# Self attention of a decoder layer: scores by 32-row query strips, probabilities turned by VectorE in 32x32 blocks, values contracted by 32 keys on four row strips

## The chip, the cores and the metric

The kernel runs on one core of one Trainium2 chip. The time is the device time of one execution in microseconds (us), median of three runs. A core has TensorE (PE in the profile, its weight loads PEld), VectorE (DVE), ScalarE (ACT), GpSimd (POOL) and SyncE (SP), which issues most DMAs. Each engine works through its own queue in order and waits on semaphores for the others.

## The reference

One post-norm decoder layer on 8 batches of 112 tokens and 256 channels, all in float32. The first third, self attention with 16 heads of 64 channels and no mask, is what changes:

```python
qkv = x @ w_qkv                                   # (8, 112, 256) @ (256, 3072)
q, k, v = split(qkv, 3)                           # 16 heads of 64
attn = softmax(einsum('bhid,bhjd->bhij', q, k) / 8)
out = einsum('bhij,bhjd->bhid', attn, v) @ w_out + b_out
x = layernorm(x + out)
```

Behind it come cross attention over 375 context rows (16 heads of 16 channels, masked), layer norm, then a mixture of 8 experts with one expert per token beside a shared one, and the last layer norm.

## The kernel before

The program is written as one instruction list for each engine; the order in a list is the order of the work, and every hand-over is a semaphore.

Self attention goes batch by batch (the loop `for b in range(B)` of each engine). Of each batch it takes 16 heads in four groups `g` of four heads; two groups, which hold the even and the odd heads of a pair of row halves, are a `pair`. On TensorE, batch `b` is, in order:

- `score1(0, b)` (L465): 8 matmuls, 64 channels by 112 queries as weights, 112 keys moving; even and odd heads use the two row halves of the array and two PSUM banks.
- from batch 2 on, `out1(b - 2)` (L504): the output projection of a tile of 128 tokens, 8 matmuls of 256 columns.
- `between1(b, 0)` and, from batch 2 on behind `score1(1, b)`, `between1(b, 1)`: two halves of the value projection of the next batch (`project_v1`, L448), each 2 matmuls of 512 columns.
- `turn(g, b)` (L477) for the four groups, with `between1(b, 2)` to `between1(b, 5)` behind each: four query/key projections for the next pair of batches (`project_qk`, L434). In batch 6 these are key and value projections of cross attention (L526, L532), in batch 7 transposes of x1, projections of cross attention's queries, values and keys (L511, L532, L518, L526).
- `value1(0, b)`, `value1(1, b)` (L491): 16 matmuls, 112 keys by 64 channels as weights, 112 queries moving.

A turn is four PE transposes of 112x112 probabilities into bank 4. All projections share banks 2 and 3 (`PE_J1`) in turns, so each waits until the bank's last content has been evacuated: value projections by ScalarE (`evac_v`, L930), query/key projections by VectorE (`evac_qk`, L1098).

On VectorE a batch is: row maxima (`rowmax`, L1105), normalisation of the probabilities with the reciprocal of their sum (`normalise`, L1111 and L1113), copies of the turned probabilities out of PSUM (`evac_pt`, L1119), the evacuations of the query/key projections, and the two parts of layer norm (`ln1_a`, L1124 to L1131, which waits for the output projection; `ln1_b`, L1139). On ScalarE a batch is: exponentials of groups 0 and 1 (`exps`, L938, four activations of 112 columns each), `evac_v(0, b + 1)`, exponentials of group 2, `evac_v(1, b + 1)`, exponentials of group 3, and two evacuations of the attended values (`evac_o`, L944).

GpSimd takes the root of the layer norm (L349) and fills constants at the start. SyncE's loads are all issued from its own list; the expert weights follow the last output projection.

A float32 matmul leaves two MATMUL and two LDWEIGHTS records in the trace, a PE transpose one.

## Time and profile before

| what | us |
|---|---|
| median of three runs (lowest, highest) | 437.46 (437.05, 437.85) |
| span of the profiled execution, first to last instruction | 436.2 |
| one batch in self attention (first score block of batch 3 to that of batch 4) | 18.55 |
| busy time of TensorE over the span | 414.0 (95%) |

The profiled execution's own time is not listed apart from its span; it is one execution of the same program as the three timed runs. Blocks of the last two batches that the next sections use, from the timeline of TensorE: a key projection 1.28 (138.32 to 139.60), a value projection of cross attention 0.98 (141.64 to 142.62), the query projection 1.54.

The page gives for each engine its busy time and share; the chain that ended last is followed back from the last instruction through whatever released each step. In the timeline each row is one or several like instructions: start, time until the last of them ended, engine, line, operation, output and inputs, shapes, and in brackets how long the engine had been idle and who ended it. A matmul's end is modelled, so the start of the next block says more on how long a block holds TensorE than its own length.

### The profile page before, as it was taken

Reading aid. Unit: us, or ns where it says so; the run is one execution under the profiler, and the core shown is the slowest. Engines: PE = TensorE matmul, PEld = TensorE weight load, DVE = VectorE, ACT = ScalarE, POOL = GpSimd, SP = SyncE. Lnnn points to the kernel's source line nnn. Section 1 sums busy time; section 2 is a strip of 40 time slices with the busy share of each in tenths; the row PEclk is TensorE's granted clock in tenths of the full one; section 3 lists DMA queues with packets and bytes.
Section 4 is the critical chain, followed back from the end, with each engine's and each line's share of the span. In section 5 each row is a group of like instructions: output and inputs, shape, how many; then the busy total and the mean of one; then the engine's idle time right before and its main releaser. Section 6 shows DMA issues by size and latency. Waiting matters only on the chain.

```text
span 436.2 us, 8958 instructions
## 1 busy us (share of the span) xinstructions
PE 414.0 (95%) x3125; PEld 297.5 (68%) x3126; DVE 243.9 (56%) x724; ACT 194.1 (45%) x580; POOL 50.9 (12%) x77
## 2 busy tenths in 40 slices
PE   8999999999999979999999999999989999999992
PEld 7767869778796856776766676767665474666661
DVE  1365765747466556666665666667762552244442
ACT  1064452433526446677666666767673101111110
POOL 4010010100101001000010101010100045212222
PEclk9999999999999999999999999999999999999999
DMA  8998100000000013040404131910000013122111
GB/s 246 365 385 242 21 2 2 0 2 2 1 2 0 2 37 145 2 181 13 170 17 166 53 130 43 387 43 2 2 2 2 1 50 109 48 62 69 67 38 31
DMA packets 15241, 34.22 MB, mean 78 GB/s; under 512 B 2381, under 2 KB 9150, under 8 KB 13920
## 3 DMA queue, kind: packets, MB, share of 16 engines
q1 hardware_dynamic: 13952, 30.70, 20.2%
q0 software_dynamic: 1104, 2.76, 1.8%
q8 instruction: 25, 0.41, 0.4%
q10 hardware_dynamic: 144, 0.23, 0.2%
q14 instruction: 16, 0.13, 0.1%
HBM read 27.24 MB, written 6.70 MB: 78 GB/s over the span
## 4 chain that ended last, share of the span: by engine, by line
PE 83%; DVE 6%; ACT 4%; issue 3%; POOL 2%; DMA 1%; POOLq 0%; DVEq 0%; ACTq 0%
PE bank L434 11%; PE bank L633 10%; PE bank L448 7%; PE bank L615 6%; PE bank L504 6%; PE bank L532 5%; PE bank L649 4%; PE bank L879 4%; PE bank L855 4%; PE bank L861 4%; PE bank L526 3%; PE bank L465 3%; PE bank L789 3%; PE bank L491 3%; PE bank L477 3%
## 5 line engine op out<-in xcount | busy, mean ns | idle before, releaser
L1234 DVE CUSTOM_DVE_ANT_0 p<-bank,mask 112x375 f32<-112x375 f32 x128 | 62.7, 545 | 36.5 <-PE bank L615 36.5
L995 ACT ACTIVATE p<-p,nm 112x375 f32<-112x375 f32 x128 | 74.8, 609 | 2.0 <-DVE nm L1234 2.0
L633 PEld LDWEIGHTS bank<-ident,p 112*125 112x125 f32 x384 | 48.9, 187 | 22.9 <-issue 14.5
L1002 ACT ACTIVATE pT<-bank 125x336 f32<-125x336 f32 x96 | 42.8, 447 | 46.0 <-PE bank L633 46.0
L633 PE MATMUL bank<-ident,p 112*125 112x112 f32 x384 | 58.8, 286 | 1.0
L434 PE MATMUL bank<-x2T,arena 128*128 128x224 f32 x256 | 54.6, 362 | 0.0
L938 ACT ACTIVATE p<-bank,nm 112x112 f32<-112x112 f32 x128 | 43.5, 365 | 18.3 <-DVE nm L1105 18.3
L434 PEld LDWEIGHTS bank<-x2T,arena 128*128 128x128 f32 x256 | 47.8, 195 | 1.0 <-DMA x2T<-in_xT 0.7
L349 POOL TENSOR_TENSOR rstd<-veps,minus_half 128x1 f32<-128x1 f32 x14 | 7.7, 549 | 292.2 <-DVE veps L1131 292.2
L1105 DVE TENSOR_REDUCE nm<-bank 112x4 f32<-112x448 f32 x32 | 19.2, 620 | 24.1 <-PE bank L465 24.1
L1098 DVE TENSOR_SCALAR arena<-bank 128x448 f32<-128x448 f32 x32 | 19.9, 623 | 22.7 <-PE bank L434 22.7
L615 PE MATMUL bank<-kT,qz 32*112 32x375 f32 x256 | 28.8, 517 | 3.6 <-ACT x2T L964 2.1
L448 PE MATMUL bank<-arena,x2T 128*112 128x512 f32 x64 | 30.2, 602 | 0.0
L944 ACT ACTIVATE arena<-bank 128x448 f32<-128x448 f32 x16 | 8.7, 544 | 48.1 <-PE bank L491 48.1
L938 ACT ACTIVATION_READ_ACCUMULATOR p<-bank,nm 112x1 f32 x128 | 27.9, 218 | 0.0
L532 PE MATMUL bank<-wx,mid 128*125 128x256 f32 x96 | 26.5, 399 | 0.0
L504 PE MATMUL bank<-arena 128*128 128x256 f32 x112 | 26.0, 385 | 0.3 <-DVE qscale L1161 0.3
L789 PE MATMUL bank<-x2T,ugs 128*128 128x512 f32 (+1 forms) x64 | 25.5, 544 | 0.6 <-DVE pT L1315 0.4
L1072 ACT ACTIVATE p<-bank 128x512 f32<-128x512 f32 x9 | 5.4, 597 | 44.9 <-PE bank L855 44.9
L649 PE MATMUL bank<-pT,v 125*32 125x112 f32 x768 | 25.0, 263 | 0.0
L649 PEld LDWEIGHTS bank<-pT,v 125*32 125x32 f32 x768 | 17.3, 109 | 10.1 <-issue 7.4
L504 PEld LDWEIGHTS bank<-arena 128*128 128x128 f32 x112 | 20.7, 190 | 4.1 <-ACT arena L944 0.5
(140 smaller groups left out, 596.5 us busy)
## 6 DMA issues: line engine op xcount, KB each, us to landing
arena<-in_ug SPq DMA_DIRECT2D x8, 1024.0 KB, 5.7
arena<-in_dn SPq DMA_DIRECT2D x8, 512.0 KB, 7.1
mid<-in_ctxT SPq DMA_DIRECT2D x8, 375.0 KB, 3.1
slots_s<-blank SPq DMA_DIRECT2D x14, 128.5 KB, 4.0
arena<-in_wqk SPq DMA_DIRECT2D x7, 256.0 KB, 5.8
slots_x<-blank SPq DMA_DIRECT2D x14, 128.0 KB, 6.1
p<-slots_s SPq DMA_DIRECT2D x9, 128.5 KB, 2.0
kT<-slots_x SPq DMA_DIRECT2D x9, 128.0 KB, 2.1
```

The source lines that it names most:

```text
L434: mm = pe.matmul(J[:, m * S_PAIR:(m + 1) * S_PAIR], wqk[:, 2 * u + m, k, :], xT[:, i, k, :], start=(k == 0), stop=(k == KC - 1))
L448: mm = pe.matmul(PE_J1[c][0:S, :], xT[:, b // 2, k, (b % 2) * S:(b % 2 + 1) * S], wv1[:, c, k, :], start=(k == 0), stop=(k == KC - 1))
L504: mm = pe.matmul(PE_W1[:, 0:C], oT1[:, k, t * TILE:(t + 1) * TILE], wout[:, k, :], start=(k == 0), stop=(k == 7))
L532: mm = pe.matmul(M[0:SK, 0:C], ctxT[:, b % 2, k, t * SK:(t + 1) * SK], wx[:, 2, k, :], start=(k == 0), stop=(k == KC - 1))
L615: mm = pe.matmul(PE_S2[r][0:S, 0:S2], qz[rows_r, b // 2 % 2, m, par, b % 2, :], kT2[rows_r, b % 2, m, :], start=True, stop=True)
L633: mm = pe.transpose(PE_T2[r][0:SK, t * S:(t + 1) * S], p2[i % RING][:, t * SK:(t + 1) * SK], ident[0:S, 0:S])
L649: mm = pe.matmul(PE_V2[VP * r:VP * r + VP, g * S:(g + 1) * S], v2[:, b % 2, t, g * STRIPS + r, :], pT2[0:SK, (n * STRIPS + r) % RING, t, : ...
L789: mm = pe.matmul(bank[2 + 2 * (n % 2) + part][:, 0:width(grp)], ugs[:, k, part * HID + m * 128:part * HID + (m + 1) * 128], x2T[:, k, grp ...
L938: e = act.activation(p1[g][:, n, :], PE_S1[g % 2][0:S, n * S:(n + 1) * S], ACT.Exp, bias=nm1[:, h:h + 1], accum_out=rs1[:, h:h + 1])
L995: act.activation(p2[i % RING], p2[i % RING], ACT.Exp, bias=nm2[:, i % H:i % H + 1], scale=-1.0).then_inc(exp2, 1)
L1002: act.activation(pT2[0:SK, i % RING], PE_T2[r][0:SK, 0:KT * S].rearrange("p (k n) -> p k n", k=KT), ACT.Copy).then_inc(pt2_act, 1)
L1234: v.tensor_tensor_reduce(p2[i % RING], PE_S2[r][0:S, 0:S2], bias[:], 1.0, 3e38, ALU.add, ALU.min, accum_out=nm2[:, i % H:i % H + 1]).then_ ...
```

## The change

Scores (`score1`): instead of one matmul per head with all 112 queries, a head gets four, one for each block of 32 queries (16 in the last). A head's strip of 32 PSUM partitions is its place among four, so a bank holds four heads by strips of 32 query rows and, side by side, the four query blocks. The two row halves of the array are used as before.

Softmax: row maxima, exponentials, reciprocals and the multiply now run over 128 partitions (four heads by 32 queries) and four query blocks, in as many instructions as before. The columns 112 to 127 of each block are zeroed once by GpSimd.

Turn: the PE transposes and the copies out of PSUM are gone. In their place VectorE transposes each group's 128x512 probabilities in 32x32 blocks from SBUF to SBUF (`turn_blocks`), with keys of a head on its strip of 32 partitions.

Values (`value1`): the contraction runs over 32 keys at a time, on four row strips of the array, accumulated over four key blocks in one PSUM bank per strip. The values are projected in the matching layout (`project_v1`): strips of 32 tokens as weights, 256 columns moving, two of four token blocks per bank; the columns of the value weights are reordered on the way in.

PSUM: the value blocks take banks 4 to 7, with the output projection in the upper half of bank 7; an evacuation of attended values reads one half of all four banks. Order on TensorE: `between1(b, 0)` moves ahead of the output projection, the turns drop out. Order on VectorE: row maxima 2 and 3 stand behind the first transpose and `normalise(1)`, and the query/key evacuations are spread between the rest (`drain1`).

The diff, cut to its core:

```diff
-        v1 = [carve(INNER)[0:S] for _ in range(2)]
+        v1 = [carve(INNER).rearrange("p (j n) -> p j n", j=QB) for _ in range(2)]
...
 
-        p1 = [p2_all[0:S, j * G1 * S:(j + 1) * G1 * S].rearrange("p (k n) -> p k n", k=G1) for j in range(4)]
-        pT1 = [pT_all[0:S, j * G1 * S:(j + 1) * G1 * S].rearrange("p (k n) -> p k n", k=G1) for j in range(4)]
+        p1_all = p2_all[:, 0:4 * QB * 128].rearrange("p (g i n) -> p g i n", g=4, i=QB)
+        p1 = [p1_all[:, g] for g in range(4)]
+        pT1 = [pT_all[:, g * QB * 128:(g + 1) * QB * 128].rearrange("p (j n) -> p j n", j=QB) for g in range(4)]
...
 
-        PE_S1, PE_J1, PE_T1, PE_U1, PE_W1 = bank[0:2], bank[2:4], bank[4], bank[5:7], bank[7]
+        PE_S1, PE_J1, PE_U1, PE_W1 = bank[0:2], bank[2:4], bank[4:8], bank[7][:, 256:512]
+        U1_ALL = banks[:, 4 * 512:8 * 512].rearrange("p (c n) -> p c n", c=STRIPS)
         PE_S2, PE_V2, PE_M2 = bank[0:STRIPS], bank[5], bank[6]
         PE_T2 = (bank[4], bank[7], PE_S2[0], PE_S2[1])
         PE_L2 = PE_S2[2]
 
-        def head1(g, n):
-
-            return 2 * G1 * (g // 2) + 2 * n + g % 2
+        def block1(j, full=True):
+
+            return SQ if full or (j + 1) * SQ <= S else S - j * SQ
...
             g.memset(ones[:], 1.0).then_inc(consts, 1)
+            g.memset(p1_all[:, :, :, S:128], 0.0).then_inc(padded1, 1)
...
             def project_v1(b, c):
+
                 if b == 0:
-                    pe.wait_ge(w_v[c], 16)
+                    for half in range(2):
+                        pe.wait_ge(w_v[half], 16)
                     pe.wait_ge(qk_sb, 7 + c)
                 elif b == 1:
                     pe.wait_ge(v1_sb, c + 1)
                     pe.wait_ge(xT_loaded[1], 16)
                 else:
                     pe.wait_ge(qk_sb, 4 * b + 3 + c)
-                for k in range(KC):
-                    mm = pe.matmul(PE_J1[c][0:S, :], xT[:, b // 2, k, (b % 2) * S:(b % 2 + 1) * S], wv1[:, c, k, :],
-                                   start=(k == 0), stop=(k == KC - 1))
+                if (b, c) == (3, 0):
+                    pe.wait_ge(prep, 7)
+                for j in (2 * c, 2 * c + 1):
+                    m = block1(j, b % 2 == 0)
+                    at = (b % 2) * S + j * SQ
+                    for k in range(KC):
+                        for strip in range(STRIPS):
+                            mm = pe.matmul(PE_J1[c][SQ * strip:SQ * strip + m, (j % 2) * 256:(j % 2) * 256 + 256],
+                                           xT[:, b // 2, k, at:at + m], wv1[:, strip // 2, k, (strip % 2) * 256:(strip % 2) * 256 + 256],
+                                           start=(k == 0), stop=(k == KC - 1))
                 mm.then_inc(v1_pe, 1)
 
...
                 cols_b = slice((b % 2) * S, (b % 2 + 1) * S)
-                for n in range(G1):
-                    for g in (2 * pair, 2 * pair + 1):
-                        h = head1(g, n)
-                        r = slice(64 * (h % 2), 64 * (h % 2) + 64)
-                        mm = pe.matmul(PE_S1[g % 2][0:S, n * S:(n + 1) * S], qT[b // 2 % 2][r, h // 2, cols_b],
-                                       kT[b // 2 % 2][r, h // 2, cols_b], start=True, stop=True)
-                        if n == G1 - 1:
-                            mm.then_inc(scores1[g], 1)
-
-            def turn(g, b):
-                if b == 0:
-                    pe.wait_ge(consts, 4)
-                pe.wait_ge(norm1, b * 4 + (g + 1))
-                if b * 4 + g >= 1:
-                    pe.wait_ge(pt1, b * 4 + g)
-                for n in range(G1):
-                    mm = pe.transpose(PE_T1[0:S, n * S:(n + 1) * S], p1[g][:, n, :], ident[0:S, 0:S])
-                mm.then_inc(turn1, 1)
+                for i in range(QB):
+                    m = block1(i, b % 2 == 0)
+                    at = (b % 2) * S + i * SQ
+                    for strip in range(STRIPS):
+                        for par in range(2):
+                            r = slice(64 * par, 64 * par + 64)
+                            mm = pe.matmul(PE_S1[par][SQ * strip:SQ * strip + m, i * 128:i * 128 + S],
+                                           qT[b // 2 % 2][r, 4 * pair + strip, at:at + m],
+                                           kT[b // 2 % 2][r, 4 * pair + strip, cols_b], start=True, stop=True)
+                            if (i, strip) == (QB - 1, STRIPS - 1):
+                                mm.then_inc(scores1[2 * pair + par], 1)
 
             def value1(pair, b):
 
-                pe.wait_ge(pt1, b * 4 + (2 * pair + 2))
+                pe.wait_ge(turned1, b * 4 + (2 * pair + 2))
                 if pair == 0:
                     pe.wait_ge(v1_sb, 2 * b + 2)
                 if b >= 1:
-                    pe.wait_ge(ot1[pair], b)
-                for n in range(G1):
-                    for g in (2 * pair, 2 * pair + 1):
-                        h = head1(g, n)
-                        col = (h // 2 % 4) * S
-                        mm = pe.matmul(PE_U1[pair][64 * (h % 2):64 * (h % 2) + 64, col:col + S],
-                                       v1[b % 2][:, h * D1:(h + 1) * D1], pT1[g][:, n, :], start=True, stop=True)
+                    pe.wait_ge(ot1[0], b)
+                    pe.wait_ge(ot1[1], b)
+                if b >= 2:
+                    pe.wait_ge(y1, b - 1)
+                for j in range(QB):
+                    n = block1(j, False)
+                    for par in range(2):
+                        at = (2 * pair + par) * D1
+                        for strip in range(STRIPS):
+                            rows_s = slice(SQ * strip, SQ * strip + n)
+                            mm = pe.matmul(PE_U1[strip][64 * par:64 * par + 64, pair * S:(pair + 1) * S],
+                                           v1[b % 2][rows_s, j, at:at + D1], pT1[2 * pair + par][rows_s, j, 0:S],
+                                           start=(j == 0), stop=(j == QB - 1))
                 mm.then_inc(pv1[pair], 1)
 
             def out1(t):
...
                     pe.wait_ge(w_loaded["out"], 16)
-                    pe.wait_ge(prep, 7)
                 else:
                     pe.wait_ge(y1, t)
...
                 score1(0, b)
+                between1(b, 0)
                 if b >= 2:
                     out1(b - 2)
-                between1(b, 0)
                 if b < 2:
                     between1(b, 1)
                 score1(1, b)
                 if b >= 2:
                     between1(b, 1)
-                turn(0, b)
-                between1(b, 2)
-                turn(1, b)
-                between1(b, 3)
-                turn(2, b)
-                between1(b, 4)
-                turn(3, b)
-                between1(b, 5)
+                for c in range(2, 6):
+                    between1(b, c)
                 value1(0, b)
                 value1(1, b)
                 if b == 1:
                     pe.wait_ge(prep, 5)
-                    pe.matmul(PE_W1[:, 0:S], anyw, ident[0:S, 0:S], start=True, stop=True).then_inc(q_any, 1)
+                    pe.wait_ge(qk_sb, 15)
+                    pe.matmul(PE_J1[0][:, 0:S], anyw, ident[0:S, 0:S], start=True, stop=True).then_inc(q_any, 1)
 
 
...
                 if n == 0 and r == 0:
-                    pe.wait_ge(pt1, 4 * B)
+                    pe.wait_ge(ot1[0], B)
+                    pe.wait_ge(ot1[1], B)
                 elif n == 0 and r == 1:
...
                     act.wait_ge(pv1[1], b - 1)
-                act.activation(v1[b % 2][:, 512 * c:512 * (c + 1)], PE_J1[c][0:S, :], ACT.Copy).then_inc(v1_sb, 1)
+                act.activation(v1[b % 2][:, 2 * c:2 * c + 2].rearrange("p j n -> p (j n)"), PE_J1[c][:, :], ACT.Copy).then_inc(v1_sb, 1)
 
             def exps(g, b):
                 act.wait_ge(max1, b * 4 + (g + 1))
                 if b >= 1:
-                    act.wait_ge(turn1, b * 4 + (g - 3))
-                for n in range(G1):
-                    h = G1 * g + n
-                    e = act.activation(p1[g][:, n, :], PE_S1[g % 2][0:S, n * S:(n + 1) * S], ACT.Exp,
-                                       bias=nm1[:, h:h + 1], accum_out=rs1[:, h:h + 1])
+                    act.wait_ge(turned1, b * 4 + (g - 3))
+                for i in range(QB):
+                    n = QB * g + i
+                    e = act.activation(p1[g][:, i, 0:S], PE_S1[g % 2][:, i * 128:i * 128 + S], ACT.Exp,
+                                       bias=nm1[:, n:n + 1], accum_out=rs1[:, n:n + 1])
                 e.then_inc(exp1[g], 1)
 
             def evac_o(half, b):
-                act.wait_ge(pv1[half], b + 1)
+                for h in range(2):
+                    act.wait_ge(pv1[h], b + 1)
                 act.activation(oT1[:, 4 * half:4 * half + 4, b * S:(b + 1) * S],
-                               PE_U1[half][:, 0:4 * S].rearrange("p (k n) -> p k n", k=4), ACT.Copy).then_inc(ot1[half], 1)
+                               U1_ALL[:, :, half * S:(half + 1) * S], ACT.Copy).then_inc(ot1[half], 1)
 
             def evac_k(m, b, J=PE_M2):
...
                     v.wait_ge(exp1[g], b)
-                v.tensor_reduce(nm1[:, G1 * g:G1 * g + G1], PE_S1[g % 2][0:S, 0:G1 * S].rearrange("p (k n) -> p k n", k=G1),
+                v.tensor_reduce(nm1[:, QB * g:QB * g + QB], PE_S1[g % 2].rearrange("p (i n) -> p i n", i=QB)[:, :, 0:S],
                                 AX.X, ALU.max, negate=True).then_inc(max1, 1)
 
             def normalise(g, b):
-                c = slice(G1 * g, G1 * g + G1)
+                c = slice(QB * g, QB * g + QB)
                 v.wait_ge(exp1[g], b + 1)
                 v.reciprocal(rc1[:, c], rs1[:, c]).then_inc(rcp1, 1)
                 v.wait_ge(rcp1, b * 4 + (g + 1))
-                v.tensor_tensor(p1[g], p1[g], rc1[:, c].unsqueeze(2).to_broadcast([S, G1, S]), ALU.mult).then_inc(norm1, 1)
-
-            def evac_pt(g, b):
-                v.wait_ge(turn1, b * 4 + (g + 1))
+                v.tensor_tensor(p1[g][:, :, 0:S], p1[g][:, :, 0:S], rc1[:, c].unsqueeze(2).to_broadcast([128, QB, S]), ALU.mult).then_inc(norm1, 1)
+
+            def turn_blocks(g, b):
+
+                v.wait_ge(norm1, b * 4 + (g + 1))
                 if b >= 1:
                     v.wait_ge(pv1[g // 2], b)
-                v.tensor_copy(pT1[g], PE_T1[0:S, 0:G1 * S].rearrange("p (k n) -> p k n", k=G1)).then_inc(pt1, 1)
+                elif g == 0:
+                    v.wait_ge(padded1, 1)
+                v.transpose(pT1[g].rearrange("p j (i a) -> p i j a", i=QB),
+                            p1[g].rearrange("p i (j a) -> p i j a", j=QB)).then_inc(turned1, 1)
 
             def layernorm_a(src, done, added, b, p, sy, ss, sa, sv):
...
                 evac_qk(n)
+            def drain1(b, c):
+
+                if b < B - 2:
+                    evac_qk(8 + 4 * b + c)
+                elif b == B - 2 and c >= 2:
+                    if c == 2:
+                        v.wait_ge(v2_ones, 2)
+                    evac_v(c - 2, 0, PE_J1[c - 2])
+                elif b == B - 1 and c == 0:
+                    evac_v(2, 0, PE_J1[0])
+                elif b == B - 1 and c == 1:
+                    evac_q(0, PE_J1[1])
+
             for b in range(B):
                 rowmax(0, b)
                 rowmax(1, b)
                 normalise(0, b)
                 if b >= 2:
                     ln1_a(b - 2)
+                turn_blocks(0, b)
+                normalise(1, b)
                 rowmax(2, b)
-                normalise(1, b)
-                if b == B - 1:
-                    evac_pt(0, b)
                 rowmax(3, b)
-                if b < B - 1:
-                    evac_pt(0, b)
-                normalise(2, b)
+                turn_blocks(1, b)
                 if b >= 2:
                     ln1_b(b - 2)
-                if b < B - 2:
-                    evac_qk(8 + 4 * b)
-                if b == B - 1:
-                    evac_v(2, 0, PE_J1[0])
-                evac_pt(1, b)
+                drain1(b, 0)
+                normalise(2, b)
+                drain1(b, 1)
+                turn_blocks(2, b)
+                drain1(b, 2)
                 normalise(3, b)
-                if b < B - 2:
-                    evac_qk(9 + 4 * b)
-                if b == B - 1:
-                    evac_q(0, PE_J1[1])
-                evac_pt(2, b)
-                if b < B - 2:
-                    evac_qk(10 + 4 * b)
-                if b == B - 2:
-                    v.wait_ge(v2_ones, 2)
-                    evac_v(0, 0, PE_J1[0])
-                evac_pt(3, b)
-                if b < B - 2:
-                    evac_qk(11 + 4 * b)
-                if b == B - 2:
-                    evac_v(1, 0, PE_J1[1])
+                turn_blocks(3, b)
+                drain1(b, 3)
                 if b == 0:
...
 
+    def by_strip(w):
+
+        return np.ascontiguousarray(w.reshape(C, 2, STRIPS, 2, D1).transpose(0, 2, 1, 3, 4).reshape(C, INNER))
```

## Rows read from the trace of the kernel before

**Rows 1.** The page: busy time by engine, granted clock by slice, the chain by engine.
```profile
PE 414.0 (95%) x3125; PEld 297.5 (68%) x3126; DVE 243.9 (56%) x724; ACT 194.1 (45%) x580; POOL 50.9 (12%) x77
...
PEclk9999999999999999999999999999999999999999
...
PE 83%; DVE 6%; ACT 4%; issue 3%; POOL 2%; DMA 1%; POOLq 0%; DVEq 0%; ACTq 0%
```

**Rows 2.** Timeline of TensorE in batch 3: start, length, engine, line, instructions.
```profile
73.15 1.04 PE L465 MATMUL bank<-arena 64*112 64x112 f32 x16
74.12 3.72 PE L504 MATMUL bank<-arena 128*128 128x256 f32 x16
77.68 1.88 PE L448 MATMUL bank<-arena,x2T 128*112 128x512 f32 x4
79.49 1.04 PE L465 MATMUL bank<-arena 64*112 64x112 f32 x16
...
82.27 0.55 PE L477 MATMUL bank<-ident,p 112*112 112x112 f32 x4
82.65 1.69 PE L434 MATMUL bank<-x2T,arena 128*128 128x224 f32 x8
...
90.02 1.75 PE L491 MATMUL bank<-pT,arena 112*64 112x112 f32 x32
91.70 0.55 PE L465 MATMUL bank<-arena 64*112 64x112 f32 x6
```

**Rows 3.** Timeline of TensorE: starts of batches 0, 2, 6, 7, cross attention.
```profile
21.71 1.04 PE L465 MATMUL bank<-arena 64*112 64x112 f32 x16
...
54.21 1.04 PE L465 MATMUL bank<-arena 64*112 64x112 f32 x16
...
128.81 1.04 PE L465 MATMUL bank<-arena 64*112 64x112 f32 x16
...
145.67 1.04 PE L465 MATMUL bank<-arena 64*112 64x112 f32 x16
...
163.21 0.90 PE L615 MATMUL bank<-kT,qz 32*112 32x375 f32 x8 [0.96 <-ACT kT L950]
```

**Rows 4.** Timeline of VectorE and ScalarE in batch 3, around its second score block.
```profile
77.88 0.42 DVE L1124 TENSOR_TENSOR ybuf<-bank,xb 128x256 f32<-128x256 f32 x1 [0.68 <-PE bank L504]
...
79.14 0.15 DVE L1131 TENSOR_SCALAR veps<-mv 128x1 f32<-128x1 f32 x1
...
80.56 0.62 DVE L1105 TENSOR_REDUCE nm<-bank 112x4 f32<-112x448 f32 x1 [1.27 <-PE bank L465]
81.10 0.17 DVE L1111 RECIPROCAL rc<-rs 112x4 f32<-112x4 f32 x1
...
81.22 0.35 ACT L938 ACTIVATE p<-bank,nm 112x112 f32<-112x112 f32 x1 [1.03 <-DVE nm L1105]
81.31 0.63 DVE L1113 TENSOR_TENSOR p<-p,rc 112x448 f32<-112x448 f32 x1
...
82.55 0.61 ACT L930 ACTIVATE arena<-bank 112x512 f32<-112x512 f32 x1
```

**Rows 5.** Timeline of TensorE in cross attention: a value block and its last round.
```profile
191.99 0.78 PE L649 MATMUL bank<-pT,v 125*32 125x112 f32 x24
...
192.50 0.28 PE L649 MATMUL bank<-pT,v 125*32 125x112 f32 x4
192.71 0.58 PE L615 MATMUL bank<-kT,qz 32*112 32x375 f32 x4
```

**Rows 6.** Groups of instructions up to 200 us: busy us, mean ns of one.
```profile
L1113 DVE TENSOR_TENSOR p<-p,rc 112x448 f32<-112x448 f32 x32 | 20.4, 638 | 1.1
...
L649 PE MATMUL bank<-pT,v 125*32 125x112 f32 x120 | 3.9, 263 | 0.0
...
L1124 DVE TENSOR_TENSOR ybuf<-bank,xb 128x256 f32<-128x256 f32 x7 | 3.0, 425 | 5.9 <-PE bank L504 5.9
```

**Rows 7.** The page: the DMA queue of instructions, packets, MB, share of 16 engines.
```profile
q8 instruction: 25, 0.41, 0.4%
```

17 lines of the change are left out of this document (10 added, 7 removed).

## The prediction

> **What bounds the kernel now.** I read the page first: TensorE (PE) is busy for 95% of the span, makes up 83% of the chain that ended last, and its granted clock stays at full speed, 2.4 GHz, in every slice [rows 1]. So in self attention the first question is TensorE's own queue. The timeline of TensorE gives one batch as a closed loop from one first score block to the next, 73.15 to 91.70, 18.55 us: scores of pair 0 0.97, output projection 3.56, value projection 1.81, scores of pair 1 and value projection 2.78, then four times a turn and a query/key projection, 7.75 together, and the values 1.68 [rows 2]. The reader is to see that these add up to the whole period: TensorE never waits there. The blocks from 21.71 to 163.21 (141.5 us) hold all eight batches; the two first take 32.50 together, batch 2 18.94, batch 6 16.86 and batch 7, with the way into cross attention, 17.54 [rows 2, 3]. The timeline of VectorE and ScalarE shows what hangs beside this: after the scores of pair 1 (79.49) the row maximum starts at 80.56, the exponentials at 81.22, and the second evacuation of values starts at 82.55, done at 83.16, in time for the second query/key projection, whose bank it frees [rows 4]. Layer norm's first part ran earlier, 77.88 to 79.29, while TensorE was still at the value projection [rows 2, 4].
>
> **The change, part by part.**
> *Turns removed.* From 82.27 to 82.65 a turn holds TensorE for 0.38 [rows 2]; four per batch are 1.5 us, 12.2 over eight batches.
> *Scores, values and value projection in tiles.* Counted in records (a float32 matmul leaves two), a pair of heads goes from 16 to 64 score records and from 16 to 64 value records, and a value projection from 4 of 512 columns to 32 of 256. What counts is how many run together. Cross attention shows it: 24 records of 125x32 (four column strips) start at 191.99, the next block follows at 192.71, and four of them started within 0.02 us, because the four together take 0.28 where one takes 0.26 [rows 5, 6]. So the 24 are six rounds of about 0.10 with four in each, and starts within a round are some 7 ns apart. With eight tiles in a round the starts would spread over 0.05, under the 0.10 of a round. Then scores are 64/8 = 8 rounds, which the 16 in pairs are now, and values 128/8 = 16 rounds, as now 32 in pairs: I take 1.01 and 1.72 (0.04 later, for the longer spread). The value projection is 8 rounds of 256 columns against 4 of 512, the same. Its price from below is 1.81; leaving a tiled block costs about 0.1 (the last round starts at 192.50 and the next block 0.21 later, against 0.10 a round [rows 5]), and I give each change of tile shape 0.1 (0 to 0.2): value projection 1.91, output projection 3.65 (it now goes into a tiled block), the first query/key projection 1.62. Bounds of the tiled blocks: below, no drain and no longer spread, 0.97 and 1.68; above, two at a time as now, 32 and 64 rounds, 3.3 a score block and 6.5 for the values. I keep to eight, since the nearest row has every tile of its round in flight (four of four).
> *VectorE.* The 32 copies of 448 columns are replaced by 32 transposes of 512 columns in 32x32 blocks. No transpose on VectorE is in the trace. A multiply of 448 columns takes 638 ns and an add of 256 takes 425 [rows 6]: 1.11 ns per column, so 512 columns at the same pace take 0.71, and the next instruction starts 0.08 sooner (80.56 to 81.10 for one of 0.62 [rows 4]): 0.63. Bounds: 0.40 if it ran at twice the pace, 1.2 at half. I take 0.63, the pace of the two nearest rows. The Trainium skill ("VectorE: DVE Perf Modes", the three transpose paths) gives 311 ns for 128 columns of bf16; with 384 columns more at 1.11 ns that is an estimate of 0.74, beside my 0.71. No run here shows it.
> *ScalarE.* The same instructions with 128 rows for 112: nothing. The output evacuation must now wait for both value blocks; only the last batch feels it.
> *Order.* This is the part that decides. The output projection now stands directly ahead of the scores of pair 1, and on VectorE layer norm's first part, a transpose and a normalisation stand ahead of row maximum 2. Let T be the start of the scores of pair 1. The output projection's result is there at T+0.20 (77.68 to 77.88), layer norm's first part takes 1.41 (77.88 to 79.29), the transpose 0.63, the normalisation 0.75 (81.10 to 81.31, and 0.54), the row maximum with the step to ScalarE 0.66 (80.56 to 81.22), four exponentials 1.33 (81.22 to 82.55), the evacuation 0.67: T+5.65 [rows 4]. Before, that evacuation was done at T+3.67. TensorE is ready for the second query/key projection at T+1.01+1.91+1.62 = T+4.54 and waits 1.1 us, since the bank is freed by that evacuation. What waits behind it on TensorE: three query/key projections, both value blocks, and all of the next batch.
> *Sum for a batch of 3 to 5.* T+5.65, three projections of 1.53 (82.65 to the next turn at 84.18, a quarter of 7.75 less 0.38) 4.59, leaving 0.10, values 1.72, scores 1.01, value projection 1.91, output projection 3.65: 18.63 against 18.55, so +0.1 each. The last transpose is done at about T+10.95, when the second value block could just start: no room there.
> *Batches 0 and 1* have no output projection and no layer norm, and both value projections stand together: 1.01 + 3.64, then the same evacuation is late by its place behind exponentials 2 (1.80 for the score block and the row maximum, +1.33+0.67 = 3.80, against 2.63 on TensorE), 4.59, 0.10, 1.72: 14.9, and 15.3 with the small mask matmul: 30.2 for 32.50, -2.3. *Batch 2:* the wait for the query scale moves from the output to the value projection; 0.0. *Batch 6* (block lengths from the table of blocks in the section on the profile): the second key projection waits for the same evacuation (T+5.57 against T+4.3), the first value projection of cross attention for a ScalarE evacuation behind exponentials 3, the last transpose for VectorE: T+11.2, with 6.6 before T 17.8 against 16.86, +0.9. *Batch 7:* the query projection waits for the x1 evacuation at T+5.35 where TensorE is ready at T+2.3; then 1.55, 1.27, a wait for VectorE, 1.27, values, and the output evacuation that needs both blocks: 18.3 against 17.54, +0.8.
> *Instruction fetch.* The queue q8 moves 0.41 MB in 25 packets [rows 7], which is 66 B for each of TensorE's 6251 records; there will be some 3700 more, 384 of them in 2.7 us at the end of each batch. Nothing bounds it below (0); above I allow 2 us in all. I take 0.3.
> Together: -2.3 + 0.0 + 0.3 + 0.9 + 0.8 + 0.3 = 0.0. The profile's span is 436.2 and the three runs are 437.05 to 437.85, so 0.9 to 1.7 lie around the span; the sum leaves both where they are: 437.4, beside a median of 437.46.
>
> **Rivals.**
> *1. The wait does not form and TensorE's sum shows.* Then a batch loses 1.53 and gains 0.04 + 0.04 + 0.04 + 0.1 + 0.1 + 0.09 + 0.1: -1.0, eight times: 429.5. For it: TensorE's 95%. Against it: the order of the queues above.
> *2. Transposes at twice the pace, 0.40.* The one ahead of row maximum 2 shortens the wait by 0.23 in six or seven batches, and batch 6 gains twice: 437.4 - 1.8 = 435.6.
> *3. Slower: the transpose takes longer than a copy per column.* Two of the four lie on the path of every batch, the first ahead of row maximum 2 and the last ahead of the second value block: sixteen in all. At 1.2 us each (+0.57): 437.4 + 9.1 = 446.5; at 0.75 it is 439.3. It decides from 0.69 on. For it: the strided block pattern on both sides, shown in no row; against it, that the rows at hand all have one pace.
> *4. Slower: eight tiles do not run together.* If four do, scores and values double their rounds: 0.77 on the first score block and 1.6 on the values, with the second score block inside the wait: +2.3 a batch, 456. The rows show four together, from column strips alone.
> The Trainium skill ("TensorE: Matmul & The Clock Gate", Part 1) states that matmul starts never come closer than about 25 ns. By that a score block would be 64 x 25 ns = 1.6 and a batch's values 3.2, close to rival 4. The trace disagrees: four starts lie within 0.02 us [rows 5].
> *5. Fetch of instructions stalls the value and score blocks*, 0.2 to 0.3 a batch: 439.5.
>
> **How the numbers follow.** Forecast 0.37, rival 1 0.05, rival 2 0.20, rival 3 0.15, rival 4 0.11, rival 5 0.12. A measurement of this kernel can tell 0.2%, 0.9 us, from no change. The forecast's own range is 436.1 to 438.7, most of it within that. Faster: rivals 1 and 2 and 0.04 of the forecast, 0.29. Same: 0.27 of the forecast and 0.03 of rival 5, 0.30. Slower: rivals 3 and 4, 0.09 and 0.06, 0.41. The range goes from rival 2 with a little beyond, 435.2, to 446, which leaves out rival 1, rival 4 and the end of rival 3, some 0.19.
>
> **What would show it.** Right: no turns on TensorE; score blocks of 64 records in 1.0 and a batch's values in 1.7; in batches 3 to 5 TensorE waits about 1.1 before the second query/key projection, with the value evacuation on ScalarE behind it and the layer norm ahead of row maximum 2; transposes of 0.7. The prediction is wrong if a transpose is far from 0.7, if the tiled blocks take more than 1.2 and 2.0, or if that wait is missing and the period of batch 4 is near 17.5.

## The result and the profile after

The changed kernel is slower: 449.60 us, median of four runs (449.01 to 450.77), against 437.25 (437.05 to 437.85, four runs beside them) for the kernel before. The ratio is 1.0295, interval 1.0278 to 1.0312. The prediction said 437.4, up to 446.0: the sum missed by 12.2 us and the range by 3.6. The profiled execution took 450.13 with a span of 448.4.

The page of the changed kernel; its rows answer to [rows 1] and [rows 7]:

```profile
PE 411.0 (92%) x4981; PEld 293.3 (65%) x4982; DVE 248.2 (55%) x724; ACT 192.6 (43%) x580; POOL 50.8 (11%) x78
...
PEclk9999999999999998999999999999999999999998
...
q8 instruction: 39, 0.64, 0.6%
...
PE 76%; DVE 8%; ACT 7%; issue 6%; POOL 2%; DMA 1%; POOLq 0%; DVEq 0%; ACTq 0%
```

TensorE is busy for less time in a longer span; VectorE, ScalarE and "issue" hold more of the chain. The timeline of TensorE in batch 3, the answer to [rows 2] (scores are L482, value projection L462, output projection L517, query/key projections L440, values L504):

```profile
73.37 0.59 PE L482 MATMUL banks<-arena 64*32 64x112 f32 x24
75.23 0.79 PE L482 MATMUL banks<-arena 64*32 64x112 f32 x40 [1.27 <-issue]
75.96 1.93 PE L462 MATMUL banks<-arena,x2T 128*32 128x256 f32 x32
77.82 3.72 PE L517 MATMUL banks<-arena 128*128 128x256 f32 x16
81.47 1.08 PE L482 MATMUL banks<-arena 64*32 64x112 f32 x64
82.48 1.93 PE L462 MATMUL banks<-arena,x2T 128*32 128x256 f32 x32
84.34 1.78 PE L440 MATMUL banks<-x2T,arena 128*128 128x224 f32 x8
87.38 4.81 PE L440 MATMUL banks<-x2T,arena 128*128 128x224 f32 x24 [1.26 <-ACT arena L939]
92.12 2.05 PE L504 MATMUL banks<-pT,arena 32*64 32x112 f32 x128
94.10 0.61 PE L482 MATMUL banks<-arena 64*32 64x112 f32 x32
```

The turns are gone, the second score block takes 1.01, and the wait in front of the second query/key projection is there, 1.26 for 1.1 forecast. What was not forecast is the hole inside the first score block: TensorE starts 24 records, stands still and waits for nothing that the profile shows ("issue"), and the block holds it for 2.59 instead of 1.01. The list of waits, 53 to 155 us (who waited for whom, us in total, times, longest), has the same:

```profile
PE banks L440 <- ACT arena L939: 5.0, 4, 1.3
PE banks L482 <- issue: 4.5, 4, 1.6
```

The first score blocks of batches 3 to 6 take 2.59, 1.98, 2.21 and 2.94: 5.7 us more than four of 1.01. From one of these four holes to the next TensorE starts some 761 records (matmuls and weight loads; 758 to 764 as the windows count them). The DMA queues in one batch (packets, MB, share), before in 91.70 to 110.26, after in 94.10 to 114.21:

```profile
q8 instruction: 1, 0.02, 0.5%
```

```profile
q8 instruction: 3, 0.05, 0.8%
```

Three packets to 761 records are some 254 records a packet. Half-microsecond windows over the hole show how one starves the engine (length, then busy time and count of PE, PEld, DVE, ACT and POOL, then granted clock, DMA share, GB/s; an instruction that crosses the edge of a window counts in both):

```profile
72.40:72.90 0.50, 0.50 (x51) 0.50 (x48) 0.21 (x1) 0.00 (x0) 0.00 (x0) 1.00 0.16 33
...
73.40:73.90 0.50, 0.50 (x27) 0.32 (x25) 0.00 (x0) 0.36 (x1) 0.00 (x0) 1.00 0.00 0
73.90:74.40 0.50, 0.06 (x4) 0.00 (x0) 0.00 (x0) 0.50 (x2) 0.00 (x0) 1.00 0.00 0
74.40:74.90 0.50, 0.00 (x0) 0.00 (x0) 0.00 (x0) 0.12 (x1) 0.00 (x0) 1.00 0.00 0
74.90:75.40 0.50, 0.17 (x15) 0.17 (x22) 0.00 (x0) 0.00 (x0) 0.00 (x0) 1.00 0.00 0
```

The packet of instructions is sent between 72.40 and 72.90, the first new records start at 75.23: over 2.3 us. The values use 256 records in 1.98 us (92.12 to 94.10 in the next batch); between 73.90 and 74.40 four matmuls that were under way end, and after them none starts until 75.23. Counted back by 256 records, the block that ran out had begun 3.6, 2.9, 3.2 and 3.8 us before the first record behind the four holes. So a block of 256 that is used up in 2 to 3 us leaves TensorE without instructions.

Further rows from the timeline of TensorE: the waits of batches 6 and 7, and the end of self attention, the answer to [rows 3].

```profile
148.91 1.53 PE L539 MATMUL banks<-mid,wx 128*128 128x375 f32 x4 [1.49 <-ACT arena L939]
...
165.05 1.78 PE L531 MATMUL banks<-x1T,wx 128*128 128x224 f32 x8 [2.81 <-ACT x1T L964]
...
173.49 0.90 PE L623 MATMUL banks<-kT,qz 32*112 32x375 f32 x8 [1.78 <-ACT kT L960]
174.32 5.38 PE L517 MATMUL banks<-arena 128*128 128x256 f32 x16
```

Behind the wait of 1.78 (0.96 before, [rows 3]) the last output projection took 5.38 where others take 3.72. The windows say why; the seventh number is the granted clock:

```profile
165.00:174.32 9.32, 7.39 (x153) 5.03 (x153) 4.01 (x9) 3.24 (x12) 0.00 (x0) 1.00 0.01 2
174.32:179.53 5.21, 5.21 (x21) 4.30 (x17) 1.96 (x8) 1.60 (x3) 0.00 (x0) 0.68 0.00 0
...
175.00:176.00 1.00, 1.00 (x4) 0.82 (x3) 1.00 (x5) 0.79 (x2) 0.00 (x0) 0.50 0.00 0
```

The clock fell to 1.2 GHz (0.50) for part of the projection; the kernel before kept 2.4 GHz there (1.00 from 165 to 175). The wait of 2.81 ends 5.23 us after the start of that batch's second score block, where the prediction had 5.35.

Last, VectorE and GpSimd in batch 3, the answer to [rows 4]:

```profile
81.58 0.42 DVE L1138 TENSOR_TENSOR ybuf<-banks,xb 128x256 f32<-128x256 f32 x1 [2.54 <-PE banks L517]
...
82.92 0.71 DVE L1132 STREAM_TRANSPOSE pT<-p 128x512 f32<-128x512 f32 x1
...
83.59 0.75 POOL L360 TENSOR_TENSOR xb<-xres,rows 128x256 f32<-128x256 f32 x1
...
83.72 1.10 DVE L1123 TENSOR_TENSOR p<-p,rc 128x448 f32<-128x448 f32 x1
```

VectorE waits 2.54 for the output projection with everything queued behind; the transpose takes 0.71, as forecast; and the second multiply of a batch takes 1.10 instead of 0.63, beside an add on GpSimd.

Periods of the batches, from one first score block to the next, read as in [rows 3]; "rest" is from cross attention's first scores to the end of the span:

| | 0+1 | 2 | 3 | 4 | 5 | 6 | 7 | rest | span |
|---|---|---|---|---|---|---|---|---|---|
| before | 32.50 | 18.94 | 18.55 | 18.55 | 18.55 | 16.86 | 17.53 | 272.96 | 436.2 |
| predicted | 30.2 | 18.9 | 18.63 | 18.63 | 18.63 | 17.8 | 18.3 | 273.0 | |
| after | 32.28 | 19.53 | 20.73 | 20.11 | 20.34 | 20.42 | 18.51 | 274.90 | 448.4 |
| e1 | 37.98 | 19.54 | 19.14 | 19.14 | 19.18 | 18.49 | 21.45 | 274.91 | 451.7 |
| e4 | 32.29 | 18.00 | 18.79 | 19.05 | 18.84 | 18.08 | 17.11 | 275.14 | 438.4 |
| e6 | 33.31 | 18.72 | 18.91 | 18.91 | 18.91 | 17.63 | 17.03 | 273.26 | 437.9 |
| e10 | 33.93 | 18.34 | 17.96 | 17.96 | 17.96 | 16.15 | 14.95 | 273.43 | 432.2 |
| e12 | 31.80 | 18.00 | 18.80 | 18.74 | 18.83 | 17.71 | 15.37 | 273.46 | 433.1 |
| e15 | 32.14 | 18.33 | 17.95 | 17.95 | 17.99 | 16.15 | 14.96 | 273.29 | 429.9 |

### The profile page after: what moved, and what is told of

It is laid out like the page before. It is cut to its first block, busy times and chain, and to the rows that moved or that the text cites. A ratio compares the mean times of both kernels' runs of the same rounds, so it can differ in the third digit from the quotient of the medians.

```text
span 448.4 us, 12670 instructions
## 1 busy us (share of the span) xinstructions
PE 411.0 (92%) x4981; PEld 293.3 (65%) x4982; DVE 248.2 (55%) x724; ACT 192.6 (43%) x580; POOL 50.8 (11%) x78
## 4 chain that ended last, share of the span: by engine, by line
PE 76%; DVE 8%; ACT 7%; issue 6%; POOL 2%; DMA 1%; POOLq 0%; DVEq 0%; ACTq 0%
PE banks L642 10%; PE banks L440 9%; PE banks L517 6%; PE banks L623 6%; PE banks L462 5%; PE banks L545 5%; PE banks L658 4%; PE banks L888 4%; PE banks L864 4%; PE banks L870 3%; PE banks L504 3%; PE banks L798 3%; PE banks L539 3%; ACT p L947 3%; PE banks L482 2%
## 5 line engine op out<-in xcount | busy, mean ns | idle before, releaser
L1245 DVE CUSTOM_DVE_ANT_0 p<-banks,mask 112x375 f32<-112x375 f32 x128 | 62.6, 544 | 36.4 <-PE banks L623 36.4
L642 PEld LDWEIGHTS banks<-ident,p 112*125 112x125 f32 x384 | 48.9, 187 | 22.9 <-issue 15.1
L947 ACT ACTIVATE p<-banks,nm 128x112 f32<-128x112 f32 x128 | 43.6, 365 | 46.5 <-DVE nm L1115 46.5
L1012 ACT ACTIVATE pT<-banks 125x336 f32<-125x336 f32 x96 | 42.8, 447 | 46.1 <-PE banks L642 46.1
L642 PE MATMUL banks<-ident,p 112*125 112x112 f32 x384 | 58.8, 286 | 1.0
L440 PE MATMUL banks<-x2T,arena 128*128 128x224 f32 x256 | 53.2, 364 | 6.9 <-ACT arena L939 6.9
L440 PEld LDWEIGHTS banks<-x2T,arena 128*128 128x128 f32 x256 | 48.5, 194 | 11.9 <-ACT arena L939 9.0
L623 PE MATMUL banks<-kT,qz 32*112 32x375 f32 x256 | 28.8, 517 | 4.5 <-ACT x2T L974 2.2
L462 PE MATMUL banks<-arena,x2T 128*32 128x256 f32 (+1 forms) x512 | 31.3, 382 | 1.2 <-issue 0.8
L947 ACT ACTIVATION_READ_ACCUMULATOR p<-banks,nm 128x1 f32 x128 | 27.9, 218 | 0.0
L517 PE MATMUL banks<-arena 128*128 128x256 f32 x112 | 27.6, 402 | 0.0
L517 PEld LDWEIGHTS banks<-arena 128*128 128x128 f32 x112 | 21.9, 201 | 5.6 <-issue 2.1
```

The source lines that it names most:

```text
L440: mm = pe.matmul(J[:, m * S_PAIR:(m + 1) * S_PAIR], wqk[:, 2 * u + m, k, :], xT[:, i, k, :], start=(k == 0), stop=(k == KC - 1))
L462: mm = pe.matmul(PE_J1[c][SQ * strip:SQ * strip + m, (j % 2) * 256:(j % 2) * 256 + 256], xT[:, b // 2, k, at:at + m], wv1[:, strip // 2, k ...
L517: mm = pe.matmul(PE_W1[:, 0:C], oT1[:, k, t * TILE:(t + 1) * TILE], wout[:, k, :], start=(k == 0), stop=(k == 7))
L623: mm = pe.matmul(PE_S2[r][0:S, 0:S2], qz[rows_r, b // 2 % 2, m, par, b % 2, :], kT2[rows_r, b % 2, m, :], start=True, stop=True)
L642: mm = pe.transpose(PE_T2[r][0:SK, t * S:(t + 1) * S], p2[i % RING][:, t * SK:(t + 1) * SK], ident[0:S, 0:S])
L947: e = act.activation(p1[g][:, i, 0:S], PE_S1[g % 2][:, i * 128:i * 128 + S], ACT.Exp, bias=nm1[:, n:n + 1], accum_out=rs1[:, n:n + 1])
```

## The experiments

Four theories were tried: that the holes are starved instruction fetch (e1, e2, e6, e8 to e10, e12 to e15); that the slow multiply counts (e3); that the order around the output projection and the layer norm costs the predicted wait and more (e4, e7); and that the end has its own cost (e5, e11). The kernel before was timed again beside each group of experiments, with medians of 436.6 to 437.1; ratios are to that.

**e1, e2: useless matmuls ahead of the first projection**, 30 in e1 (120 records) and 64 in e2 (256 records).

```diff
+            for i in range(30):
+                r = 32 * (i % 4)
+                pe.matmul(PE_M2[r:r + 32, 0:32], blank[:, 0:32], blank[:, 0:32], start=True, stop=True)
```

> The changed kernel with 30 useless small matmuls (32x32 weights, 32 columns, four column strips, 120 records of TensorE) ahead of the first projection; nothing else. In the changed kernel TensorE stands still inside the score block that follows the values, 1.53, 0.92, 1.24 and 1.83 us in batches 3 to 6, at records 761 apart, where a batch has 736 to 744. Theory A (instruction blocks): instructions arrive in blocks of 256, a block is ordered when the one before it is begun, and it takes about 3.3 us; a run of 256 records that TensorE finishes in less waits for the rest. 120 records more move the block edges to before the values, into the query/key projections, or to the end of the scores: the four standstills go, 5 us less, about 444.5. Rival B (the standstill belongs to the hand-over from the tiled values to the tiled scores, or to PSUM): it stays at its place, and the time is 449.6 or 0.5 more for the extra matmuls.

> The same with 64 useless matmuls, 256 records, a whole block. Theory A: the block edges lie where they lay, the standstills of 0.9 to 1.8 us in the score blocks of batches 3 to 6 come back, 449.6 to 450.5. Rival B: also unchanged. If instead the extra instructions at the start helped by something else (a warmer start, another phase against the loads), this one would be as fast as the one with 120 records.

e1: 452.70 (451.49 to 455.14), ratio 1.0363 [1.0320, 1.0407]. e2: 449.53 (448.43 to 451.47), 1.0279 [1.0257, 1.0301]. In e1 the holes of batches 3 to 6 are gone, and batches 3 to 5 take 19.14 to 19.18. The first score block of batch 4 is whole:

```profile
98.53 1.08 PE L482 MATMUL banks<-arena 64*32 64x112 f32 x64
```

In e2 they are back in the same four blocks, behind the same matmul of each (24, 37, 49 and 62 of 64), so exactly 256 records on. Batch 3 of e2:

```profile
75.54 0.59 PE L482 MATMUL banks<-arena 64*32 64x112 f32 x24
76.85 0.79 PE L482 MATMUL banks<-arena 64*32 64x112 f32 x40 [0.72 <-issue]
```

A hole that stays with a shift by 256 records and goes with one by 120 depends on blocks of 256 instructions, so it is the fetch. The early holes say the same: in the changed kernel, e1, e4, e7, e9, e10, e13 and e14 the first one stands 437 to 440 records from the start, whatever work lies there.

The time of e1 was missed: 444.5 was expected, and it rose by 3.1. In its profile batches 3 to 6 are 5.7 shorter, as expected, but batches 0 and 1 are 5.7 longer: while the weights are loaded (323 GB/s over the first 40 us of the changed kernel), holes of 3.1, 1.7 and 2.6 us came up. Batch 7 is 2.9 longer, of which 1.1 is a further hole, 0.5 lies in its values and 1.3 is the clock, granted at 0.61 and 0.80 over the two blocks behind a wait of 2.91.

**e3: GpSimd's add waits for the end of row maximum 3, the batch's last**, so that it no longer runs beside the multiply (`g.wait_ge(max1, 4 * t + 4)` ahead of L360).

> The changed kernel, where GpSimd's sum of input and bias (128x256) waits in addition for row maximum 3 of its batch. In the changed kernel the second normalising multiply of VectorE took 1.10 us in place of 0.63 in batches 3 to 6, each time beside that sum of GpSimd. Theory: the two share a way to the on-chip memory; with the sum moved, the multiply takes 0.63 and the exponentials of group 2 start 0.47 earlier in five batches: -2.4 us, 447.2. Rival: the multiply is slow because it follows a transpose; then it stays at 1.1 and the time is the same.

449.79 (446.74 to 451.10), 1.0304 [1.0282, 1.0326]. The multiply is back at 0.62, still behind a transpose, so the rival is out:

```profile
80.96 0.62 DVE L1124 TENSOR_TENSOR p<-p,rc 128x448 f32<-128x448 f32 x1
```

In the profile batches 3 to 6 are 0.45 us each shorter (sum 79.81 for 81.60), but that was the fastest of the five runs, and the median does not show it.

Cause and cure of the slow multiply are shown; that it is worth 2 us of the whole is not.

**e4: the layer norm's first part behind row maximum 3 on VectorE**, nothing else.

```diff
                 normalise(0, b)
-                if b >= 2:
-                    ln1_a(b - 2)
                 turn_blocks(0, b)
                 normalise(1, b)
                 rowmax(2, b)
                 rowmax(3, b)
+                if b >= 2:
+                    ln1_a(b - 2)
```

> The changed kernel with the first part of layer norm behind row maxima 2 and 3 on VectorE, instead of ahead of the first transpose. Theory (the order on VectorE makes the wait before the second query/key projection): row maximum 2 starts about 2.4 us earlier after the second score block, the wait of 1.3 us before the second query/key projection goes, and the slow multiply is no longer between. 1.3 in batches 3 to 5, up to 1.5 in batches 6 and 7: about -8 us, 441.5, with the standstills in the score blocks left. Rival (the wait only moves to the last transpose, since VectorE has the same work): values start as late as before, under 2 us gained, 448.

439.35 (437.27 to 440.68), 1.0052 [1.0034, 1.0070]: 10.2 us less than the changed kernel, by the place of four small instructions of VectorE in each of six batches. The wait in front of the second query/key projection is gone, also the one of batch 6; the holes stay (1.2 to 1.7, measured as above by the length of the score block less 1.01; the brackets give less). Batch 4:

```profile
92.05 0.60 PE L482 MATMUL banks<-arena 64*32 64x112 f32 x27 [1.04 <-issue]
...
100.97 6.32 PE L440 MATMUL banks<-x2T,arena 128*128 128x224 f32 x32
107.22 2.12 PE L504 MATMUL banks<-pT,arena 32*64 32x112 f32 x128
```

**e7: the other way to the same end**, the output projection again ahead of the first value projection on TensorE (`out1(b - 2)` before `between1(b, 0)`), VectorE as in the changed kernel.

> The changed kernel with one part undone: the output projection of a token tile stands again ahead of the first value projection on TensorE, as before the change; VectorE's order is that of the changed kernel. Theory (VectorE's first layernorm instruction waits 2.5 us for the end of the output projection, and transposes, row maxima and drains queue behind it; the projection now ends 1.93 us earlier): the wait is 0.5 to 0.7 us, the one in front of the second query/key projection (1.24) goes or halves, batches 3 to 6 are about 1.0 shorter each and batch 7 0.5: about 445. The fetch standstills (0.9 to 1.8) are at another place in the block, as 1.7 us of long matmuls stand between scores and value projection now, and smaller if the fetch has caught up: down to 442. Rival (the layernorm's place on VectorE matters through its own 1.2 us, not through what it waits for): 449.

440.87 (440.10 to 443.69), 1.0106 [1.0076, 1.0136]: 8.7 less, nearly twice the 4.6 that were expected, and below the 442 given as the least. VectorE's wait fell from 2.54 to 0.65; the holes stay, in the same records as before.

```profile
96.17 0.43 DVE L1138 TENSOR_TENSOR ybuf<-banks,xb 128x256 f32<-128x256 f32 x1 [0.65 <-PE banks L517]
```

So one wait for one late result costs 8.7 to 10.2 us, and either order takes it away; the change had moved both sides at once.

**e5: e4, and in the last batch the keys' drains ahead of the output's on ScalarE. e11: that edit alone in the kernel before.**

```diff
-                evac_o(0, b)
                 if b == B - 1:
                     evac_k(0, 1, PE_J1[0])
                     evac_k(1, 1, PE_J1[1])
+                evac_o(0, b)
                 evac_o(1, b)
```

> The layernorm's start behind the fourth row maximum, as in e4, and in the last self-attention batch ScalarE drains the two key tiles of the cross attention before the two halves of the attention output instead of between them. Theory (an end effect that the prediction did not price: TensorE stood 1.78 us in front of the first cross-attention scores, and its granted clock was then 0.5 to 0.65 for some 3.5 us, so that the output projection took 4.80 us instead of 3.72): the wait falls to about 1.0, as before the change, the projection takes 3.7 to 3.8 and the clock stays at 1.00; 1.8 to 2.0 us less than e4's 439.35, that is 437.4. Rival (the clock falls because the eight-tile values ahead of it count for little, not because of the wait): the wait shrinks, the clock still falls, 438.5. The instruction-fetch standstills of batches 3 to 6 (1.1 to 1.6 us each) stay where they are under both.

> The kernel before with the key drains of the last batch ahead of the output's drains on ScalarE, e5's second edit alone, as its control: TensorE waited 0.96 us for them in front of cross attention's first scores (its clock stayed at 1.00 there). Theory (the wait is the drains' place): 0.5 to 0.9 shorter, 436.4; then half of what e5 won over e4 (2.1 us) was open to the kernel before too, and the rest was the clock. Rival (the output projection's own wait for the output's second drain takes its place): 437.1, no change.

e5: 437.24 (435.11 to 439.41), 1.0002 [0.9983, 1.0020], 2.1 less than e4. The wait is gone, the projection is back at 3.72, the clock at 1.00:

```profile
161.43 0.90 PE L623 MATMUL banks<-kT,qz 32*112 32x375 f32 x8
162.63 3.72 PE L517 MATMUL banks<-arena 128*128 128x256 f32 x16 [0.30 <-ACT arena L954]
```

e11: 435.33 (434.83 to 436.50), 0.9973 [0.9960, 0.9987], 1.3 less than the kernel before. So more than half of e5's gain was open to the kernel before too. The rest is put down to the clock, which in e4 cost some 1.7 over the first scores and the projection (6.04 for 4.38 in e6, at 1.00); the split was not measured more closely.

**e6: e4 with the tile runs spread.** The values of pair 0 move behind the second of four query/key projections, the output projection ahead of the value projection; no instruction more or less.

```diff
                 score1(0, b)
-                between1(b, 0)
                 if b >= 2:
                     out1(b - 2)
+                between1(b, 0)
...
                 for c in range(2, 6):
                     between1(b, c)
-                value1(0, b)
+                    if c == 3:
+                        value1(0, b)
                 value1(1, b)
```

> e4's kernel with the short tile instructions spread out: the values of the first pair of groups are contracted behind the second of the four query/key projections instead of behind the fourth, and the output projection stands again between the scores and the value projection. No instruction is added or removed. Fetch theory (256 instructions of 16 KB run out faster than the 3.3 us that the next block takes): at most 128 + 128 tile records follow each other without a long matmul between, so the standstills inside the score block of batches 3 to 6 (1.12, 1.30, 1.26, 1.63) are under 0.4 each, batches 3 to 6 come to some 17.6 us, and the time is 4 to 5 us under e4's 439.35, about 434.7, which is under the kernel before (436.6). Rival (VectorE's chain sets the batch, the standstills only fill its waits): the standstills go, but waits for VectorE or ScalarE take their place, batches stay at 18.8 to 19.0, 439. Rival 2 (the standstill is not the fetch but the turnover from the values' banks): standstills stay where they are, 439.

441.24 (439.61 to 445.29), 1.0125 [1.0092, 1.0157]. Both halves of the outcome were on record with different theories: from batch 2 on all holes are gone, as the fetch theory says, and the time did not fall (it rose by 1.9), as the rival says. A wait took their place, 0.69 in batches 2 to 5 and 1.22 in batch 6; batch 4:

```profile
109.97 1.13 PE L504 MATMUL banks<-pT,arena 32*64 32x112 f32 x64 [0.69 <-DVE pT L1133]
```

VectorE had itself waited 1.48 in front of the third query/key drain, with the last normalisation and transpose queued behind it.

**e9: e6, that queue mended** (`normalise(3, b)` and `turn_blocks(3, b)` ahead of `drain1(b, 2)`), with e5's edit. **e10: e9 with the value projection ahead of the output projection again.**

> e6's spread order with its new wait taken away: on VectorE the last normalisation and transpose of a batch stand ahead of the third query/key drain (in e6 the second value block waited 0.69 us for that transpose in batches 2 to 5 and 1.22 in batch 6, while VectorE itself had idled 1.48 in front of the drain), and the key drains first in the last batch as in e5. Theory (e6 turned the fetch standstill into a wait for VectorE; both away leave TensorE's own sum, 17.8 and some 0.4 for a second values block's end and the wait for the output's drain): batches 3 to 5 take 18.2 to 18.3 (e6: 18.91), batch 6 16.5, no standstill over 0.35 us from batch 2 on, no clock below 1.00 near 165: 441.24 - 2.7 - 1.2 - 1.8 = 435.5. Rival (ScalarE's or VectorE's queue gives another wait): 437 to 438.

> e9 with the value projection again ahead of the output projection, so that three tile blocks (values of the second pair, scores, value projection, 384 records in some 4 us) follow each other behind the long query/key projections. Fetch theory: the records behind the second block's edge are asked for about 1 us after the first edge is crossed and come 3.3 us after it, so a standstill of 0.2 to 0.8 comes back in some of batches 3 to 6, in the score block or the value projection: 0.5 to 2 us over e9, 436 to 437.5. Rival (the long value projection hides the fetch: 0.95 us for 64 records at 15 ns each): as e9 or, as the drain of the first value block starts earlier, 0.3 under it.

e9: 433.31 (433.10 to 434.81), 0.9927 [0.9914, 0.9941]. e10: 432.47 (430.99 to 433.98), 0.9899 [0.9881, 0.9917]. Both beat the kernel before, and e11, its version with the keys first, by 2.0 and 2.9 us. e9's batches 3 to 5 take 18.15 (18.2 to 18.3 expected), its time is 2.2 under the 435.5 expected. A batch of e10 has no wait at all; its period is TensorE's own sum:

```profile
91.78 1.08 PE L482 MATMUL banks<-arena 64*32 64x112 f32 x64
92.78 1.93 PE L462 MATMUL banks<-arena,x2T 128*32 128x256 f32 x32
94.64 3.72 PE L517 MATMUL banks<-arena 128*128 128x256 f32 x16
98.30 1.08 PE L482 MATMUL banks<-arena 64*32 64x112 f32 x64
99.30 1.93 PE L462 MATMUL banks<-arena,x2T 128*32 128x256 f32 x32
101.17 3.29 PE L440 MATMUL banks<-x2T,arena 128*128 128x224 f32 x16
104.39 1.13 PE L504 MATMUL banks<-pT,arena 32*64 32x112 f32 x64
105.45 3.29 PE L440 MATMUL banks<-x2T,arena 128*128 128x224 f32 x16
108.67 1.13 PE L504 MATMUL banks<-pT,arena 32*64 32x112 f32 x64
```

The hole that the fetch theory expected for e10 did not come: its three tile blocks in a row take 3.9 us, nearly half of it in the slower value projection.

**e12: e10 with the values together again**, the one edit undone.

> e10 with one edit undone: both value blocks of a batch stand together again behind the fourth query/key projection, directly ahead of the next scores (192 matmuls in three tile blocks in a row, where e10 has 64 ahead of the scores). Same instructions, and VectorE and ScalarE in e10's order. Fetch theory (a block of 256 records takes 3.3 us from the edge crossed to the first record started, and values with scores use 256 up in some 3.1): the standstills of 1.0 to 1.6 us inside the score blocks of batches 3 to 6 return at the places of e4 and e5, their periods are 18.8 to 19.0 instead of 17.96, and the time is 4 us over e10: 436.5. Rival (e10's gain over e5 came from VectorE's order): it stays within 1 us of e10, 432.5 to 433.5.

435.59 (433.21 to 436.80), 0.9982 [0.9968, 0.9995]: 3.1 over e10, and the holes are back at the very records of e4, e5 and the changed kernel. The rival is out: VectorE's order was e10's. (The spans in the table differ by only 0.9: the profiled run of e10 was its slowest, with a hole in batch 0. Batches 2 to 7 are 4.1 longer in e12.)

```profile
88.99 0.79 PE L482 MATMUL banks<-arena 64*32 64x112 f32 x37
90.52 0.60 PE L482 MATMUL banks<-arena 64*32 64x112 f32 x27 [0.74 <-issue]
```

**e13, e14, e15: e10 with e1's useless matmuls**, 15, 30 and 45 of them, to see whether e10 was lucky with the edges of its blocks.

> e10 with 15 useless 32x32 matmuls (60 records, some 0.4 us) ahead of the first projection: every later instruction lies 60 records further in the fetched blocks. Theory 1 (e10 is free of standstills by its order: no 256 records in a row take less than the 3.3 us of a block's turnaround, save values, scores and value projection together): periods of batches 3 to 5 stay within 0.3 of 17.96, time 432.9 and up to 2 us more from the load phase. Theory 2 (it is the place of the edges: an edge at the start of the second value block leaves 2.1 us of value and score records and part of a value projection ahead of the next): with some of the three shifts standstills of 0.5 to 1 come in each batch, 435 to 437.

> e10 with 30 useless matmuls (120 records). Theory 1: batches 3 to 5 at 17.96 within 0.3, 433.3 and up to 3 us more from the load phase, where e1's shift by as much met standstills of 3.0, 1.6 and 2.5 us. Theory 2: the edge falls near the start of the second value block here, so this is the shift with the largest standstill, 0.5 to 1 a batch in batches 3 to 6, 437.

> e10 with 45 useless matmuls (180 records). Theory 1: batches 3 to 5 at 17.96 within 0.3, 433.7 and up to 3 us more from the load phase. Theory 2: the edge lies inside the query/key projections ahead of the second value block, standstills under 0.4 a batch, 434.

435.82 (434.02 to 436.42), 437.21 (433.69 to 438.10) and 432.53 (431.71 to 432.87); ratios 0.9975 [0.9961, 0.9989], 1.0000 [0.9977, 1.0023], 0.9907 [0.9886, 0.9928]. Batches 3 to 5 take 17.95 to 17.99 in all three, but for one of 18.24 (e14, 0.3 in a value projection): the order keeps them free in all four places of the edges that were tried. Batches 0 and 1 are another matter: 35.61 in e13 and 36.20 in e14 for 33.93 in e10, with holes of 2.5 and 1.4 (e13) and 2.8 and 1.7 us (e14), where e10 has one of 1.9; e15 has none. Through these holes the times of e13 and e14 come out at theory 2's 435 to 437, but not by its mechanism: the periods are theory 1's. e15 lies 1.2 under the least that theory 1 gave it. Batch 0 of e14:

```profile
22.16 0.59 PE L482 MATMUL banks<-arena 64*32 64x112 f32 x24
25.24 0.81 PE L482 MATMUL banks<-arena 64*32 64x112 f32 x40 [2.50 <-issue]
```

**e8: the kernel before with the scores alone in 32-query tiles.**

```diff
-                    for g in (2 * pair, 2 * pair + 1):
+                    for i in range(4):
+                        m = min(32, S - 32 * i)
+                        at = (b % 2) * S + 32 * i
+                        for g in (2 * pair, 2 * pair + 1):
...
```

> The kernel before with one part of the change alone: the scores computed by query blocks of 32 rows (64 tile matmuls of 64 rows by 32 columns a pair of groups instead of 16 of 64 by 112), written where the kernel before has them; softmax, transposes and values as before. Theory (the tiles themselves cost what the long ones do, eight at a time, and only runs of more than 256 records without a long matmul starve): a score block takes 1.0 to 1.1 us as before, a batch has 192 records more but no dense run over 128, so no standstill in batches 3 to 6; in the first 35 us, when fetches took 6 to 18 us, one or two standstills of 0.5 to 2 us: 437.5, between 436.6 and 439. Rival (any extra instructions cost their fetch, about 1.3 us per 256): 96 x 16 more records x 2, that is 12 blocks more than before at 0.5 to 1.3 us each, 443 or more.

437.33 (436.58 to 438.31), 1.0011 [1.0001, 1.0021]. A score block takes 0.99, a batch 18.60 for 18.55. Six more packets (31 for 25; the rival had counted twelve) cost next to nothing where no dense run needs them: records are not what costs, but their rate.

```profile
91.08 1.06 PE L468 MATMUL bank<-arena 64*32 64x112 f32 x64
92.07 3.72 PE L507 MATMUL bank<-arena 128*128 128x256 f32 x16
```

## Why the prediction was wrong, step by step

*Tiles: right.* Eight run together. Score blocks 1.01 (forecast 1.01), value projection 1.86 (1.91), output projection 3.65. The values were mis-sized: 1.98 from their start to the next block instead of 1.72, 0.26 a batch, 2.1 us in all. Rival 4 is out, and so is the Trainium skill's 25 ns between matmul starts ("TensorE: Matmul & The Clock Gate", Part 1): 64 records start within 1.01 us, 16 ns each.

*VectorE: right.* A transpose 0.71. Rivals 2 and 3 are out.

*Order: the mechanism was right, and dear.* The wait is 1.26 at T+5.91, forecast 1.1 at T+5.65 (T 81.47, projection 87.38); the slow multiply alone, 1.02 from its start to the next where the sum had 0.54, is more than the difference. e4 and e7 show what this step held: without it 10.2 and 8.7 us come back. The forecast had it as the reason that nothing would be gained. That is half of the reason: e4 is without the wait and still gains nothing over the kernel before, until the holes are gone too (e9, e10).

*Instruction fetch: the step that failed.* "I take 0.3", with 2 us as the upper bound. The score blocks behind the values lose 5.7 us in batches 3 to 6, and the two value projections of batches 0 and 1, 4.77 and 4.27 us where e15's first pair takes 3.69, add 1.7: 7.3. Rival 5 had the mechanism and the place; its 439.5 holds 2 of the 7.3 us. The step divided bytes, and though it counted 384 records in 2.7 us it never asked how long one block lasts: 256 records are used up in 2 to 3 us there, and the next block's first record came 2.9 to 3.8 us after the block before it was begun. The size of a block stood on the page: 25 packets to 6251 records are 250 records a packet.
The Trainium skill ("Runtime: NRT & Kernel Launch", Instruction fetch mechanics) says that the queue is refilled in blocks of 256 instructions while the current one executes, and that crossing a block is "mostly hidden". The 256 agree with e2's shift; mostly hidden holds for the kernel before and for e8, not for the changed one.

*The end: not priced.* The evacuation that needs both value blocks was forecast (batch 7 18.3, measured 18.51). What came behind it was not: the granted clock at 0.68 over the next projection, 5.21 us where e6 takes 3.55. The rest is 1.9 longer.

The terms by period add up: batches 0 and 1 +2.1 over the forecast, batch 2 +0.6, batches 3 to 5 +5.3, batch 6 +2.6, batch 7 +0.2, rest +1.9, less the 0.3 that was taken for fetch: 12.4, for 12.2 measured. In batches 3, 4 and 5 the holes explain 1.58, 0.97 and 1.20, the late second projection 0.26 each and the values 0.26 each: 5.3. Batch 6 is 1.93 of hole, 0.26 of values and some 0.4 of waits at the key and value projections; batch 2, without a hole, has the other two terms, 0.5 of its 0.6. e1 is the check: without holes its batches 3 to 5 take 19.14 to 19.18, which is the forecast 18.63 and twice 0.26. Of the 12.2 us, then, 7.0 are fetch beyond the 0.3, 2.1 the values, 1.4 the later second projection and the waits of batch 6, and 1.7 the clock.

Rival 1, that the wait does not form and TensorE's sum shows, was given 429.5. Its mechanism is e10 and e15, where batches 3 to 5 gain 0.6 and not 1.0, mainly because the two value blocks take 2.12 together where the sum had 1.72.

Open: whether the weight loads are what makes the holes of the first 35 us longer; the holes of e1, e13 and e14 are only seen together with them, and moving the loads was not tried. Open too is the exact rule of the fetch: counted by records, e15 goes from one edge to the next in some 2.2 to 2.9 us around its second value blocks and shows no hole there. And what decides when the clock falls is open, as the last section shows.

## What to carry to other kernels

Cutting a matmul into many tiles that run together cost little time on the array here (scores 1.01 for 0.97, values 1.98 for 1.68), but it multiplies the rate at which instructions are used: look for stretches of some 250 TensorE records in under 3 us, which are at risk, and put long matmuls between them. When an order is rewritten, follow each late result to everything that is queued behind its reader: one add on VectorE, waiting for one projection, was worth 10 us over the six batches that have it. A version without a standstill may still show no gain until the wait that took its place is moved too (e6 against e9, where some 2 of the 7.9 us are e5's edit).

## What the runs showed of the hardware

- TensorE stands still for instructions, marked "issue": in the changed kernel 1.0 to 1.9 us at a time in batches 3 to 6 (0.7 to 1.6 in the brackets), in e1 up to 3.1 in the first 30 us. In e2, 256 records more move the holes by 256 records exactly.
- After a wait of 1.78 us behind a 2.05 us block of small tiles, the clock was granted at 0.68 over the next 5.2 us, so partly at 1.2 GHz. e4 shows the same (projection 4.80), e5, without the wait, does not. But e2 and e6 had such a wait with the clock at 1.00, so the wait alone does not decide it. In e1, e2 and e3 the clock also fell one wait earlier, behind the 2.8 to 2.9 us for x1 in batch 7 (granted 0.86 and 0.64 over the next two blocks of e2, 5.92 us for 4.61); in the changed kernel and e7 it stayed at 1.00 there.
- VectorE's multiply of 448 columns with two inputs in SBUF takes 1.10 us beside GpSimd's add and 0.62 without (e3). In e4 it hits a subtract and multiply with one tensor input (L1153) instead, 0.82 for 0.36. The Trainium skill ("SBUF — State Buffer", SBUF: two separate sides) gives the two engines one shared pair of ports under an exclusive lock; the trace agrees that they hold each other up, but does not show whether by a lock.
- A 32x32-block transpose of 128x512 float32 on VectorE, SBUF to SBUF: 0.71 us.
